# Twenty products of values, and the steps at which they stand: fifteen cycles of a hybrid attention kernel with another table

## The reference

```python
gl_v = (x @ Ws).reshape(b, t, h, e)                       # 8 heads, e = 5 experts
wv = _topk_mask(gl_v, SEL) * jax.nn.sigmoid(gl_v)         # two of five, per token and head
xv = jnp.einsum('btd,edk->btek', x, Wv)
v = jnp.einsum('bthe,btek->bhtk', wv, xv)                 # the values: a sum of five products
scores = jnp.einsum('bhid,bhjd->bhij', q * scale, k)
probs = jax.nn.softmax(scores, axis=-1)
attn = jnp.einsum('bhij,bhjd->bihd', probs, v)
```

## Time and profile before

| | us |
|---|---|
| time, median of 3 runs | 1936.66 |
| lowest and highest | 1934.22, 1939.07 |
| the profiled execution, its own time | 1933.94 |
| its span, first to last instruction | 1932.2 |
| PE busy | 1784.0 (92%) |
| DVE busy | 1582.3 (82%) |
| ACT busy | 1261.5 (65%) |
| POOL busy | 1032.9 (53%) |

### The profile page before, as it was taken

One profiled execution on the slowest core, in us unless ns is written; L12 is line 12 of the kernel. 1 busy time (PEld: TensorE's weight loads), 2 busy tenths in 40 slices (PEclk: granted clock), 3 DMA queues, 4 the chain that ended last, 5 costly groups with the idle time before them and its releaser, 6 DMA issues.

```text
span 1932.2 us, 32178 instructions
## 1 busy us (share of the span) xinstructions
PE 1784.0 (92%) x11200; PEld 891.0 (46%) x11200; DVE 1582.3 (82%) x2962; ACT 1261.5 (65%) x2774; POOL 1032.9 (53%) x1122
## 2 busy tenths in 40 slices
PE   4888999999999999999999999999999999999997
PEld 2343544535454453545445454454545445354444
DVE  5477888988888898888989888898888889887775
ACT  1537667585766757677675766758576675857654
POOL 1415475563737556374664637466464755736453
PEclk7769999999999999999999999999999999999989
DMA  3110011110101111011111101111110111100000
GB/s 107 50 48 26 26 42 39 31 48 25 34 31 46 39 31 48 12 40 39 46 39 31 42 18 40 39 45 39 32 32 28 40 39 32 48 12 15 12 11 6
DMA packets 87481, 67.92 MB, mean 35 GB/s; under 512 B 10632, under 2 KB 83016, under 8 KB 87240
## 3 DMA queue, kind: packets, MB, share of 16 engines
q1 hardware_dynamic: 86914, 65.47, 11.3%
q10 hardware_dynamic: 408, 0.39, 0.1%
HBM read 31.76 MB, written 8.39 MB: 21 GB/s over the span
## 4 chain that ended last, share of the span: by engine, by line
PE 48%; DVE 39%; ACT 9%; issue 3%; POOL 0%; SPq 0%; DMA 0%; DVEq 0%; ACTq 0%; POOLq 0%
DVE nmaxA L988 9%; PE Y L553 8%; DVE ztmp L1106 6%; DVE nmaxF L993 5%; ACT Pq L808 4%; PE S1c L489 4%; PE S2a L513 4%; PE S1b L489 4%; PE Y L543 4%; PE S2b L513 4%; PE M L606 3%; DVE nmaxA L983 3%; DVE ztmp L1078 3%; PE M L660 2%; DVE beaten_by L1052 2%
## 5 line engine op out<-in xcount | busy, mean ns | idle before, releaser
L1275 POOL TENSOR_TENSOR Z<-Z,ztmp 128x1280 f32<-128x1280 f32 (+1 forms) x110 | 316.5, 2878 | 340.2 <-DVE ztmp L1106 339.6
L1240 POOL TENSOR_SCALAR_AFFINE_SELECT PT<-PT 128x256 f32<-128x256 f32 (+1 forms) x640 | 258.0, 414 | 296.3 <-ACT PT L793 291.9
L1265 POOL TENSOR_TENSOR Vf<-Vf,ztmp 128x512 f32<-128x512 f32 x240 | 317.8, 1324 | 83.9 <-DVE ztmp L1078 79.6
L793 ACT ACTIVATE PT<-S2a 128x512 f32<-128x512 f32 x320 | 191.6, 599 | 130.3 <-PE S2a L507 128.3
L553 PE MATMUL Y<-PT,Vf 128*64 128x512 f32 x1024 | 268.0, 614 | 0.0
L1078 DVE TENSOR_TENSOR ztmp<-xv,wv_s 128x512 f32<-128x512 f32 x240 | 243.8, 1016 | 0.0
L797 ACT ACTIVATE PT<-S2a 128x512 f32<-128x512 f32 x256 | 153.2, 598 | 129.3 <-PE S2a L513 125.6
L489 PE MATMUL S1c<-Kf,Qf 64*128 64x512 f32 x352 | 201.8, 654 | 32.5 <-ACT Pq L808 31.4
L489 PE MATMUL S1a<-Kf,Qf 64*128 64x512 f32 x352 | 200.4, 649 | 25.5 <-ACT Pq L808 25.5
L793 ACT ACTIVATE PT<-S2b 128x512 f32<-128x512 f32 x320 | 191.5, 598 | 30.6 <-PE S2b L507 30.6
L489 PE MATMUL S1b<-Kf,Qf 64*128 64x512 f32 x320 | 183.3, 653 | 13.0 <-ACT Pq L808 10.7
(11 more groups left out here) (134 smaller groups left out, 3735.4 us busy)
## 6 DMA issues: line engine op xcount, KB each, us to landing
Qs<-parts SPq DMA_DIRECT2D x96, 128.0 KB
Ks<-parts SPq DMA_DIRECT2D x93, 128.0 KB
tab_s<-in_tab SPq DMA_DIRECT2D x16, 512.0 KB, 4.4
out_x<-res SPq DMA_DIRECT2D x31, 256.0 KB, 2.4
xr<-out_x SPq DMA_DIRECT2D x24, 256.0 KB, 2.9
wa_s<-in_wa SPq DMA_DIRECT2D x16, 320.0 KB, 3.2
xl<-in_x SPq DMA_DIRECT2D x8, 256.0 KB, 3.1
Qs<-mrowA SPq DMA_DIRECT2D x128, 4.0 KB, 1.8
```

Of the source, the lines that this page charges most:

```text
L793: nc.scalar.activation(PT[:, slot % 2, b, :], t[:, :], ACT.Exp, scale=SCALE_A).then_inc(exps_done.sem, 1)
L1265: nc.gpsimd.tensor_tensor(Vf[:, i, :, :], Vf[:, i, :, :], vtmp_of(j, n), ALU.add).then_inc(v_acc.sem, 1)
L1275: nc.gpsimd.tensor_tensor(Z[:, own, :, :], Z[:, own, :, :], ztmp[:, hh % 2, own, :, :], ALU.add).then_inc(z_acc.sem, 1)
```

## The change

The table of products gets other steps, and the lookup is written so that a step may hold two products. A product is still at the step of its place in the table.

```diff
-        V_STEPS = [(s, b) for s, bs in ((1, (8, 9)), (2, (1, 3, 5, 8)), (3, (0, 2, 4, 7)), (4, (0, 1, 3, 4, 5, 6, 7)),
-                                        (5, (0, 1, 2)))
+        V_STEPS = [(s, b) for s, bs in ((1, (8, 9)), (2, (1, 3, 5, 5)), (3, (1, 3, 7)), (4, (0, 1, 3, 4, 5, 6, 7, 9)), (5, (0, 1, 2)))
                    for b in bs]
...
-                        if at in v_steps(j) and f:
-                            f_value_product(*divmod(v_steps(j).index(at), E))
+                        for n in (n for n in range(NT * E) if at == v_steps(j)[n]):
+                            if f:
+                                f_value_product(*divmod(n, E))
...
-                        if at in v_steps(j) and f:
-                            f_value_sum(*divmod(v_steps(j).index(at), E))
+                        for n in (n for n in range(NT * E) if at == v_steps(j)[n]):
+                            if f:
+                                f_value_sum(*divmod(n, E))
```

## The result

| | before | changed |
|---|---|---|
| median (us) | 1935.44 (4 runs) | 1956.67 (4 runs) |
| lowest to highest | 1933.94 to 1939.07 | 1955.99 to 1956.78 |
| span of the profiled execution | 1932.2 | 1955.0 |

The ratio is 1.0103, 95% interval 1.0087 to 1.0119: slower by 1%, 21 us. The forecast was 10.4 us slower, 1947.0 us, with a range of 1936 to 1957. The way and the mechanism at slots 3 and 5 were right; half of the size was missing, and the measured time lies at the very end of the range. One run of the later kernel with (4, 6) free took 2230.17 us at a granted clock of 0.74, a slow state of the chip; its ratio is without that run.

What follows compares the result with a forecast made beforehand. No engine alone bounds it: PE's work is strung up by maximum, exponential and next score matmuls. Loss 1.54 less gain 0.85, times 15, is + 10.4 us; on 1933.94, plus 2.7 for the median, 1947.0 us; range 1936 to 1957.

Steps and rivals of the forecast that it cites:

- the mechanism at slots 3 and 5: Slot 3's maxima start earlier, gaining 0.85 us; slot 5's maximum 0 waits for product 16, losing 1.54 us.
- Product 5 costs nothing at (2, 5): Behind product 4, DVE had 0.86 us idle and the product needs 0.60 us; at worst some 0.1 us.
- Gain at slot 3, 0.85 us: Slot 3's pair of steps 4 and 5 starts at 860.50, not 861.35; bounds 0.30 and 1.96 us.
- Who earns the gain: In slot 3, product 6 no longer lies between maxima 0 and 1, so maximum 1 starts 1.9 us earlier.
- Loss at slot 5, 1.54 us: Product 14's sum runs before product 16; slot 5's maximum 0 is 1.67 us later, its steps 2 and 3 1.54.
- Per cycle + 0.69 us: Loss 1.54 less gain 0.85 us in each of 15 changed cycles, the last counted alike: + 10.4 us.
- Behind it PE has 12.47 us of work in 12.50, nothing that swallows it: In slot 5, from 885.50 to 898.00, PE is nearly always busy, so the 1.54 us loss stays.
- a rival in which the gain at slot 3 shrinks to 0.30 us: Exponential 2 late or POOL's masks hold the `Y` matmuls: 1.24 us a cycle, + 18.6 us, 1955.3 us; chance 0.10.
- The prediction's own case: Gain 0.85 at slot 3 and loss 1.54 us at slot 5, 1947.0 us, range 1942 to 1953; chance 0.62.

Runs made afterwards that it cites:

- later kernel with (4, 6) free: Against the changed kernel: products 8, 9, 10 at (3, 4), (3, 7), (3, 8), six products in slot 4, none at (4, 6); 1928.62 us, ratio to before 0.9950.
- product 5 alone: The kernel before with only product 5 moved, from (2, 8) to (2, 5); 1926.22 us, ratio 0.9935.
- short sums: GpSimd's sums cut to one head of eight, values incomplete, in both kernels: kernel before 1933.07 us, changed kernel 1925.38 us.
- slot 3 alone: New order of slots 2 and 3, product 9 at (3, 8), products 10 to 19 as in the kernel before; 1924.67 us, ratio 0.9933.
- slots 4 and 5 alone: Slots 4 and 5 as in the changed kernel, the rest as before except product 9, from (3, 7) to (4, 0); 1966.21 us, ratio 1.0153.
- filled kernel: The changed kernel with the four transposes of slot 5, step 1 done three times over in cycles up to 16; 1948.25 us, ratio to before 1.0058.
- product 16 behind maximum 0: The changed kernel with product 16 at (5, 0), behind maximum 0 of slot 5, in place of (4, 9); 1941.75 us, ratio to before 1.0023.

## Why the prediction was right in its way, and short in its size

- *Product 5 costs nothing at (2, 5).* Right: 0.26 us of idle time left, and the maximum behind it not later.
- *Gain at slot 3, 0.85 us.* Right in each step: 0.30 us at the first pair, the second wait gone. Measured 0.95. The 0.1 us is the overlap of PE's rows: I let the pair of steps 4 and 5 start at the shown end of the `Y` matmuls, and it starts 0.07 us ahead of it.
- *Who earns the gain.* The prediction gave part of it to product 6 moving behind maximum 1, since that lets maximum 1 come 1.9 us earlier. It came earlier, but product 5 alone wins the same: it lets product 6 finish ahead of `rest1`.
- *Loss at slot 5, 1.54 us, by the sum between products 15 and 16.* Right to the hundredth: product 16 took 1.75 us, the wait rose from 0.23 to 1.77 us. With short sums product 16 took 0.68 us.
- *Per cycle + 0.69 us.* Measured + 0.60. The last changed cycle was counted alike; it had no gain at slot 3 and a wait longer by 1.92 us.
- *What was missing.* The step "Behind it PE has 12.47 us of work in 12.50, nothing that swallows it" priced that work at the clock of before. In 6 of 14 cycles it began at the lower level, 1.64 us more each time, 9.8 us in the execution. The size of the sum was off by this term, with the last changed cycle (1.9 us, counted as 0.7) and the end of the program (3.4 us) beside it. The 3.4 us are PE's work in cycle 17 at a mean granted clock of 0.84 in place of 0.87. They are no part of the loss described here: the kernels with product 5 alone and with slot 3 alone, which are faster than before, have nearly the same end (94.3 us behind the last start of a slot 2, in place of 91.5, and the same clock of 0.84), and the one with slots 4 and 5 alone does not (91.5 us, 0.87). What sets the clock there isn't shown.
- *The range held by luck.* No case of the prediction had the clock in it. The range reached up to 1957 for a rival in which the gain at slot 3 shrinks to 0.30 us, 1955.3 us; the gain did not shrink. The prediction's own case had the range 1942 to 1953, and the measured 1956.67 lies outside it.

Why the clock falls behind this wait in some cycles and not in others, which have the same rows, stays open. That the falls come with the wait is shown by the filled kernel and by the three others without the long wait (slots 2 and 3 alone, product 5 alone, product 16 behind maximum 0), none of which has a fall in a full cycle. Which length is enough was not tried, and length alone does not decide: with slots 4 and 5 alone the last changed cycle has a fall behind 1.99 us, in the changed kernel it has none behind 2.00, and with short sums one fall came behind 1.38.

## What to carry to other kernels

Ask for each moved instruction which maximum, or other head of a chain, stands right behind it, and whether the other engine has an addition pending at that moment: two products in a row let the waiting sum in between them, and the second then costs 1.75 us, not 0.68. A table of places can hold a gain and a loss of like size; try its entries one by one. Here one entry alone, product 5 behind product 4, makes the kernel 0.65% faster than before, and all the others together turn that into 1% slower. The part that loses is what puts two products ahead of maximum 0 of slot 5. Count a new idle time of TensorE twice: once as time, and once for the clock behind it.

## What was not expected of the hardware

- A wait of TensorE of 1.77 us, with PE busy on both sides of it, was followed in 6 of 14 cycles by matmuls at 1.2 GHz (granted clock 0.54 over the 3.62 us behind it), and in 8 by none, in a program whose cycles repeat to a few hundredths of a us. Waits of 1.38 us were followed by none in the 14 full cycles of the kernel before, and by one in the 14 of the same kernel with short sums. The Trainium skill, page "TensorE: Matmul & The Clock Gate", section "Part 1: The HAM clock gate (the "warmup" mystery)", says that the throttled state is the default and that activity releases it; the rows agree in that each fall in the full cycles of the changed kernel stands behind this idle time.
- Work that computes nothing new made the kernel faster: 0.87 us of repeated transposes inside the wait of each cycle saved 8.4 us in all.
